# An attention and feed-forward kernel on one core: transposes moved next to scores, sums of two head pairs issued together

## What is computed

```
x = x + attn_a(layernorm(x))     # sigmoid projections Q, K, V; weights A from the means of Q and K; A @ V @ Wo + bo
x = x + ffn(layernorm(x))        # (silu(x Wg^T) * (x Wu^T)) Wd^T, hidden 384, weights are int32 times 1/127
x = x + attn_b(layernorm(x))     # 16 heads of 64, below
x = x + ffn(layernorm(x))        # the same weights again

# attn_b, per batch and head
q, k, v = x Wq + bq, x Wk + bk, x Wv + bv          # [256, 64] each
pattern = softmax(causal(q k^T / 8))               # [256, 256], upper triangle masked
out    += (pattern v) Wo                           # plus bo once
```

## Time and profile before

| what | value |
|---|---|
| runs of before | 382.17, 383.46, 384.61 us; median 383.46 us |
| the profiled execution | 382.15 us, of which 380.3 us is the span from first to last instruction |
| PE busy | 344.0 us, 90% of the span, 3208 matmuls |
| weight loads (PEld) | 277.0 us, 73% |
| DVE, ACT, POOL busy | 273.7 us (72%), 231.4 us (61%), 204.6 us (54%) |
| chain that ended last | PE 80%, DVE 6%, POOL 5%, issue 4%, ACT 2%, DMA 2% |
| mean granted TensorE clock | 0.971 of full speed |

### The profile page before, as it was taken

How to read it: one execution, slowest core, us unless ns; L and a number is a source line. 1 busy time by engine, 2 the same in 40 slices (tenths; PEclk the granted TensorE clock), 3 DMA queues, 4 the chain that set the end, 5 groups by cost and what they waited for, 6 DMA issues and landing times.

```text
span 380.3 us, 9882 instructions
## 1 busy us (share of the span) xinstructions
PE 344.0 (90%) x3208; PEld 277.0 (73%) x3208; DVE 273.7 (72%) x1084; ACT 231.4 (61%) x784; POOL 204.6 (54%) x273
## 2 busy tenths in 40 slices
PE   0366699999999999999999999999999999999865
PEld 0265578777877788778878788778887867787654
DVE  1344588897688877886888688887778697767533
ACT  2233357877486758765867658574866476658601
POOL 1616685575468635772578247753574275517420
PEclk9978899999999999999999999999999999999985
DMA  7500000000000000000000000000000000000000
GB/s 275 162 0 0 3 1 3 1 2 3 3 2 0 3 2 2 16 1 2 3 16 2 3 2 3 16 0 2 3 14 4 0 3 16 1 2 3 16 15 14
DMA packets 6418, 5.82 MB, mean 15 GB/s; under 512 B 864, under 2 KB 5856, under 8 KB 6368
## 3 DMA queue, kind: packets, MB, share of 16 engines
q1 hardware_dynamic: 5936, 3.62, 3.3%
q10 hardware_dynamic: 432, 1.57, 1.1%
HBM read 4.15 MB, written 1.05 MB: 14 GB/s over the span
## 4 chain that ended last, share of the span: by engine, by line
PE 80%; DVE 6%; POOL 5%; issue 4%; ACT 2%; DMA 2%; ACTq 0%; POOLq 0%; DVEq 0%
PE bank L380 11%; PE bank L224 10%; PE bank L359 8%; PE bank L294 7%; PE bank L346 7%; PE bank L308 7%; PE bank L344 6%; PE bank L225 6%; PE bank L226 6%; PE bank L284 4%; PE bank L285 3%; PE bank L242 2%; PE bank L273 2%; DMA wqkv<-wqkv_in 2%; POOL wqkv_lo L697 1%
## 5 line engine op out<-in xcount | busy, mean ns | idle before, releaser
L710 POOL TENSOR_TENSOR prob<-prob,row_inv 128x256 f32<-128x256 f32 (+1 forms) x128 | 103.1, 827 | 103.1 <-DVE row_inv L627 103.1
L471 ACT ACTIVATE prob<-neg_s,neg_max 128x256 f32<-128x256 f32 x128 | 63.9, 499 | 0.0
L478 ACT ACTIVATE prob_t<-bank 128x384 f32<-128x384 f32 x64 | 31.5, 492 | 39.5 <-PE bank L359 38.9
L613 DVE CUSTOM_DVE_ANT_0 neg_s<-bank,mask 128x256 f32<-128x256 f32 x128 | 53.4, 417 | 0.0
L637 DVE TENSOR_TENSOR qk<-bank,bqk 128x512 f32<-128x512 f32 x64 | 43.9, 686 | 10.2 <-PE bank L226 10.0
L469 ACT ACTIVATE prob<-neg_s,neg_max 128x128 f32<-128x128 f32 x128 | 50.6, 395 | 0.0
L620 DVE COPY prob_t<-bank 128x384 f32<-128x384 f32 x64 | 35.5, 554 | 18.9 <-PE bank L359 18.5
L380 PE MATMUL bank<-prob_t,v 128*64 128x256 f32 (+1 forms) x512 | 48.9, 332 | 0.0
L380 PEld LDWEIGHTS bank<-prob_t,v 128*64 128x64 f32 x512 | 31.8, 136 | 19.5 <-issue 10.0
L224 PE MATMUL bank<-rt_hi,wqkv_hi 128*128 128x256 f32 x128 | 42.5, 332 | 1.0 <-DVE rt_lo L586 0.9
L359 PEld LDWEIGHTS bank<-ident,prob 64*128 64x128 f32 x768 | 28.9, 138 | 14.9 <-issue 10.3
(11 more groups left out here) (135 smaller groups left out, 781.9 us busy)
## 6 DMA issues: line engine op xcount, KB each, us to landing
wqkv<-wqkv_in ACTq DMA_DIRECT2D x3, 512.0 KB, 5.4
x<-x_in SPq DMA_DIRECT2D x8, 128.0 KB, 5.7
out<-x SPq DMA_DIRECT2D x8, 128.0 KB, 1.8
wo<-wo_in SPq DMA_DIRECT2D x1, 512.0 KB, 4.7
wa<-wa_in SPq DMA_DIRECT2D x1, 192.0 KB, 6.8
wg_i<-wg_in SPq DMA_DIRECT2D x1, 192.0 KB, 5.8
wu_i<-wu_in SPq DMA_DIRECT2D x1, 192.0 KB, 5.8
wd_i<-wd_in SPq DMA_DIRECT2D x1, 192.0 KB, 5.9
```

The lines of the kernel that those rows point to most:

```text
L471: nc.scalar.activation(prob[:, r, e, P:SC], neg_s[:, m % 2, e, P:SC], ACT.Exp, bias=neg_max[:, q, 2 * e + 1:2 * e + 2], scale=-1.0, accum_ ...
L613: nc.vector.tensor_tensor_reduce(out=neg_s[:, m % 2, e, P:SC], in0=S[:, P:SC], in1=mask[:], scale=-SCORE_SCALE, scalar=3e38, op0=ALU.add, ...
L710: nc.gpsimd.tensor_tensor(pr, pr, inv, ALU.mult).then_inc(p_norm, 1)
```

## The change

The transposes of m move on PE to the scores of m+2 (2.045 instead of 2.693 in the table): for an odd m they follow these scores directly, for an even m one `sum` stands between. Scores get two PSUM banks of their own and transposes two; the ring and the waits that it needed are gone. The sum of an odd step m does the matmuls of m-1 and m together, and the result takes a turn in bank 1 of G (`take("sum", m)`) where it had z_ps to itself; `pv_done` and `z_sb` become that bank's full and free counts. All times in the tables are drawn anew, so side jobs move by some places, and so does which bank of G a job uses. For steps 24 to 26 the order on PE becomes

The number of matmuls, their shapes, and the work of the other engines are unchanged. The diff (left out are most rows of JOBS):

```
--- before.py
+++ after.py
@@ -33,7 +33,6 @@
 FC = F // P
 U = H // 2
 LAST = B * U
-LAG = 2
 SC = N + P
 HALF = 512
 HALVES = (slice(0, A), slice(A, P))
@@ -46,44 +45,44 @@
 
 
 HEADS = {
-    "PE": {"qk": -1.278, "scores": 0.0, "transposes": 2.693, "sum": 3.069},
-    "ACT": {"exp1": 0.39, "exp0": 0.465, "pt0": 2.199, "z": 2.767},
-    "DVE": {"qk": -1.106, "mask": 0.271, "inverse": 1.471, "pt1": 2.768},
-    "POOL": {"norm": 3.377},
+    "PE": {"qk": -1.313, "scores": 0.0, "transposes": 2.045, "sum": 3.01},
+    "ACT": {"exp1": 0.471, "exp0": 0.639, "pt0": 1.988, "sum": 2.727},
+    "DVE": {"qk": -0.869, "mask": 0.53, "inverse": 1.577, "pt1": 2.671},
+    "POOL": {"norm": 4.775},
 }
 JOBS = {
...
-    "POOL": {"lnsA": -13.523, "sv": -10.311, "stdp": -8.267, "lnsF": -6.527, "lnsB": -2.301, "bo": 8.947, "lnsP": 16.052},
...
+    "POOL": {"lnsA": -12.191, "sv": -7.951, "stdp": -6.381, "lnsF": -4.946, "lnsB": -1.068, "bo": 9.541, "lnsP": 16.209},
 }
 ONCE = {
-    "PE": {"bo": -7.196},
-    "ACT": {"w0": -19.802, "w1": -17.798, "w3": -14.741, "w5": -10.773, "w2": -5.195, "w4": -4.286},
-    "DVE": {"bv": -12.471, "bo": -6.68},
-    "POOL": {"w0": -22.399, "w1": -12.777, "w2": -2.943, "w3": -1.872, "w4": 0.687, "w5": 2.435},
+    "PE": {"bo": -8.324},
+    "ACT": {"w0": -18.328, "w1": -15.329, "w3": -13.411, "w4": -11.381, "w5": -9.462, "w2": -8.193},
+    "DVE": {"bv": -8.887, "bo": -3.165},
+    "POOL": {"w0": -22.179, "w1": -12.109, "w5": -4.077, "w2": -1.805, "w3": -0.176, "w4": 2.76},
 }
-BANK = {"qk": 0, "lntA": 3, "qkv0": 0, "qkv1": 1, "qkv2": 3, "mean": 2, "vwo": 1, "aout": 2, "lntF": 2, "gF0": 2, "gF1": 3, "gF2": 1,
-        "dnF": 2, "lntB": 2, "v0": 0, "v1": 1, "v2": 1, "v3": 3, "bo": 3, "out0": 1, "out1": 3, "lntP": 3, "gP0": 2, "gP1": 3, "gP2": 0,
-        "dnP": 3}
+BANK = {"qk": 0, "sum": 1, "lntA": 1, "qkv0": 3, "qkv1": 1, "qkv2": 2, "mean": 3, "vwo": 3, "aout": 2, "lntF": 3, "gF0": 2, "gF1": 3,
+        "gF2": 1, "dnF": 2, "lntB": 2, "v0": 2, "v1": 1, "v2": 1, "v3": 3, "bo": 0, "out0": 3, "out1": 2, "lntP": 3, "gP0": 1, "gP1": 3,
+        "gP2": 2, "dnP": 2}
 
 
 EARLY = ("lnsA", "lntA", "qkv0", "qkv1", "qkv2", "sv", "mean", "dist", "sign", "stdp", "vwo", "aout", "lnsF", "lntF", "gF0", "gF1", "gF2", "dnF")
-START = [0, 7.97, 16.07, 24.07, 32.01, 40.05, 48.03, 56.07]
+START = [0, 8.1, 16.07, 24.08, 32.07, 40.04, 48.03, 56.06]
 
 
 def order(engine):
 
     steps = []
     for name, at in HEADS[engine].items():
-        steps += [((m | 1 if name == "sum" else m) + at, name, m) for m in range(LAST)]
+        steps += [(m + at, name, m) for m in range(LAST) if name != "sum" or m % 2]
     for name, at in JOBS[engine].items():
         steps += [((START[b] if name in EARLY else U * b) + at, name, b) for b in range(B)]
     for name, at in ONCE[engine].items():
@@ -152,7 +151,7 @@
         zt = sb("zt", [P, 2, U, N])
 
         bank = [ctx.enter_context(nc.psum_tensor(f"bank{i}", [P, 512], F32)) for i in range(8)]
-        ring, z_ps, G = bank[0:3], bank[3], bank[4:8]
+        s_banks, t_banks, G = bank[0:2], bank[2:4], bank[4:8]
 
 
         ld_x = [sem(f"ld_x{b}") for b in range(B)]
@@ -172,7 +171,7 @@
 
         s_full, s_masked, p_inv, p_norm = sem("s_full"), sem("s_masked"), sem("p_inv"), sem("p_norm")
         p_exp = [sem("p_exp0"), sem("p_exp1")]
-        pt_full, pt_sb_a, pt_sb_b, pv_done, z_sb = (sem(n) for n in ("pt_full", "pt_sb_a", "pt_sb_b", "pv_done", "z_sb"))
+        pt_full, pt_sb_a, pt_sb_b = (sem(n) for n in ("pt_full", "pt_sb_a", "pt_sb_b"))
         stored = sem("stored")
 
         def full(eng, job, n):
@@ -185,12 +184,6 @@
 
         def home(job):
             return G[BANK[job]], g_full[BANK[job]], g_free[BANK[job]]
-
-        def s_bank(m, e):
-            return ring[(4 * m + e) % 3]
-
-        def t_bank(m, e):
-            return ring[(4 * (m + LAG) + 2 + e) % 3]
 
         def queries(m, h):
 
@@ -302,7 +295,7 @@
                     last.then_inc(done, 1)
                 elif job in ("out0", "out1"):
                     j = int(job[3])
-                    pe.wait_ge(z_sb, U // 2 * (b + 1))
+                    freed(pe, "sum", U * (b + 1) - 1)
                     take(job, b)
                     for u in range(U):
                         last = nc.tensor.matmul(out[:, 0:D], zt[:, b % 2, u, j * P:(j + 1) * P], wo[:, u, :], start=(u == 0), stop=(u == U - 1))
@@ -337,51 +330,49 @@
                 freed(pe, "qk", m)
                 if m:
                     pe.wait_ge(s_masked, 2 * m)
-                if m > LAG:
-                    pe.wait_ge(pt_sb_a, m - LAG)
                 r = m % 3
                 for e, half in enumerate(HALVES):
-                    nc.tensor.matmul(s_bank(m, e)[:, 0:P], qk[half, r, 0, 0:P], qk[half, r, 1, 0:P], start=True, stop=True)
+                    nc.tensor.matmul(s_banks[e][:, 0:P], qk[half, r, 0, 0:P], qk[half, r, 1, 0:P], start=True, stop=True)
                 for e, half in enumerate(HALVES):
-                    nc.tensor.matmul(s_bank(m, e)[:, P:SC], qk[half, r, 0, P:N], qk[half, r, 1, :], start=True, stop=True).then_inc(s_full, 1)
+                    nc.tensor.matmul(s_banks[e][:, P:SC], qk[half, r, 0, P:N], qk[half, r, 1, :], start=True, stop=True).then_inc(s_full, 1)
 
             def transposes(m):
 
                 pe.wait_ge(p_norm, 2 * m + 2)
                 if m:
+                    pe.wait_ge(pt_sb_a, m)
                     pe.wait_ge(pt_sb_b, m)
-                if m + LAG < LAST:
-                    pe.wait_ge(s_masked, 2 * (m + LAG) + 1)
                 for e in range(2):
                     for j in range(3):
                         for h, half in enumerate(HALVES):
                             at = (3 * e + j) * A
-                            last = nc.tensor.transpose(t_bank(m, h)[:, at:at + A], prob[half, m % 3, e, j * P:(j + 1) * P], ident[half, half])
+                            last = nc.tensor.transpose(t_banks[h][:, at:at + A], prob[half, m % 3, e, j * P:(j + 1) * P], ident[half, half])
                             if e == 1 and j == 2:
                                 last.then_inc(pt_full, 1)
 
-            def weighted_sum(m):
+            def weighted_sums(m):
 
                 b, u = divmod(m, U)
+                out, done, _ = home("sum")
                 pe.wait_ge(pt_sb_a, m + 1)
                 pe.wait_ge(pt_sb_b, m + 1)
-                if u == 0:
+                if u == 1:
                     freed(pe, "v0", b)
                     freed(pe, "v1", b)
-                if u == U // 2:
+                if u == U // 2 + 1:
                     freed(pe, "v2", b)
                     freed(pe, "v3", b)
-                if m % 2 == 0 and m:
-                    pe.wait_ge(z_sb, m // 2)
-                t = m % 2 * N
-                for k, cols in ((0, slice(0, N)), (1, slice(N, SC))):
-                    for e, half in enumerate(HALVES):
-                        h = 2 * u + e
-                        last = nc.tensor.matmul(z_ps[half, t + k * P:t + N], v[:, b % 2, k, h * A:(h + 1) * A], prob_t[:, m % 4, e, cols],
-                                                start=(k == 0), stop=(k == 1), skip_group_check=True)
-                last.then_inc(pv_done, 1)
-
-            steps = {"scores": scores, "transposes": transposes, "qk": projections, "sum": weighted_sum}
+                take("sum", m)
+                for i in (m - 1, m):
+                    t = i % 2 * N
+                    for k, cols in ((0, slice(0, N)), (1, slice(N, SC))):
+                        for e, half in enumerate(HALVES):
+                            h = 2 * (i % U) + e
+                            last = nc.tensor.matmul(out[half, t + k * P:t + N], v[:, b % 2, k, h * A:(h + 1) * A], prob_t[:, i % 4, e, cols],
+                                                    start=(k == 0), stop=(k == 1), skip_group_check=True)
+                last.then_inc(done, 1)
+
+            steps = {"scores": scores, "transposes": transposes, "qk": projections, "sum": weighted_sums}
             for name, n in order("PE"):
                 if name in steps:
                     steps[name](n)
@@ -441,7 +432,7 @@
                     src, _, free = home(job)
                     full(act, job, b)
                     if b >= 2:
-                        act.wait_ge(pv_done, U * (b - 1))
+                        full(act, "sum", U * (b - 1) - 1)
                     nc.scalar.activation(v[:, b % 2, j, g * HALF:(g + 1) * HALF], src[:], ACT.Copy).then_inc(free, 1)
                 elif job[0] == "w" and job != "vwo":
                     i = int(job[1])
@@ -474,25 +465,25 @@
             def pt_evac(m):
                 act.wait_ge(pt_full, 2 * m + 1)
                 if m >= 4:
-                    act.wait_ge(pv_done, m - 3)
-                nc.scalar.activation(queries(m, 0), t_bank(m, 0)[:, 0:SC].rearrange("p (k s) -> p k s", s=A), ACT.Copy).then_inc(pt_sb_a, 1)
+                    full(act, "sum", m - 4 | 1)
```

(38 more changed lines are left out.)

63 lines of the change are left out of this document (28 added, 35 removed), and 6 rows, old and new, of the table JOBS.

## The result

The changed kernel takes 368.8 us (368.5 to 371.21, 4 runs), before 384.03 us in the same comparison: a ratio of 0.962 (95% interval 0.956 to 0.968). In a second comparison it took 371.22 us beside 383.22, a ratio of 0.967 (0.963 to 0.972). The forecast was 371 us, with a range of 368.5 to 378. The profiled execution took 371.21 us, the slowest of its four, with a span of 369.4.

What follows compares the result with a forecast made beforehand. PE was taken as busy throughout, bound by what it issues, including 0.15 to 0.19 us per change of form. Savings of 13.2 us less 0.5 and 0.3 gave 12.4, so 383.46 became 371 us; range 368.5 to 378.

Steps and rivals of the forecast that it cites:

- The tolls: On PE, 44 fewer entries into whole-array form save 8.4 us and 32 fewer into transposes 4.8, together 13.2 us.
- step 0 and misfits: Costs set against the saving: 0.5 us for transposes0 waiting for norm0, 0.3 us for small misfits in 60 steps.
- the masks: PE's waits for masks between first and last scores: 0.6 us at most would go, taken as 0.
- The seam: Passage on PE from scores directly to transposes: 0.06 us at the lower end, 0.21 at the upper; the lower was taken.
- The rival with the bare weight loads: Transposes' weight loads, 0.139 us each, lie bare after scores, so 4.8 us stay: 375.9 us; chance 0.09.
- transposes25: Tightest place for PE behind norm in a period: margin 1.3 us, or 0.7 if a gate job delays DVE; cost 0.
- transposes28: Among steps 27 to 31 of a period, said to leave 1.1 us or more behind norm; cost 0.
- the walk: The new order laid against durations for one period, to find margins of transposes behind norm; cost 0.
- Both rivals with late norms: Transposes wait for POOL every period: one norm late, 383.5 us, chance 0.07; two late, 396 us, chance 0.05.
- the one with bank 1: DVE at gF2 and ACT at copies 0.7 us later, PE stalls, 6 us lost: 377 us; chance 0.10.
- From scores63 on: The kernel's end, bound by latency: sum62 waits for a copy, other jobs offset it; net 0, between -0.5 and +1.
- The start: Up to scores0: sv.1 goes behind lnsB.0 and a weight split on POOL; scores0 stay at 48.7 us, within 0.5.

## Why the prediction was right

**The tolls.** The mechanism was right: 8.4 + 4.8 us were forecast for 44 and 32 changes of form fewer, and the job put between shows what they cost. From the first to the last scores before took 302.72 us and after 290.36: 12.4 us less, to the tenth what was forecast. That precision is luck, since two terms were off by as much in opposite directions. PE's busy time fell by 11.7 us (301.47 to 289.76) and not by 13.2. Its idle time fell by 0.65 us (1.25 to 0.60), where 0.8 more had been put down for step 0 and misfits and nothing for waits that go. One of those waits the prediction didn't count at all; it gave the masks as the only one in these 303 us, but before had a second:

```profile
PE bank L242 <- POOL xn_F L672: 0.4, 1, 0.4
```

In a period the tolls gave 1.61 us and not 1.74. Of that 0.13 us the new order costs 0.11 in every period at one place: `qk` now stands right behind `mean`, whose last matmuls (L250) have one column, and its first matmul costs 0.23 us for 0.12. Before, scores stood there and cost their usual 0.42.

```profile
183.61 0.34 PE bank L250 x4
183.95 0.23 PE bank L217
```

The seam was taken at its lower end, 0.06, and the chain shows 0.37 for twelve transposes. The rival with the bare weight loads (375.9 us) is refuted by that piece.

**Waits.** (The times of this paragraph are differences of starts and ends in the trace of the kernel after.) Transposes behind norm cost 0.5 us at step 0 and nothing after, as forecast. At transposes25, told as the tightest place, norm ended 1.0 us ahead (forecast 0.7 to 1.3). In truth transposes28 are tighter, 0.65 us where I had told 1.1 or more: still enough, but the walk was off by half a microsecond there, and it is this step and those like it where putting all sums last ran dry. Both rivals with late norms, and the one with bank 1, are out by PE's single line of waits. The runs show that they weren't idle fears: with half of the transposes 1.45 us earlier, waits for norm (7.9 us) and for the later copies (4.4 us) take back what was gained there, and a poorly chosen bank costs 17.8 us of waiting.

**Small items.** From scores52 to scores63: 46.55 us before, 44.41 after, 2.1 less. Six entries into the whole array and five into transposes fewer make 1.9; PE's busy time fell by 1.6 and 0.6 of idle time went. From scores63 on: 28.86 before, 27.68 after in the profile, 29.0 in the second profile of the same kernel, so the 0 that was forecast holds within what executions of one kernel differ by. The start was told as 48.7 give or take 0.5, and it came at 51.36 and 50.68 us. That step was too narrow: I saw sv.1 behind the weight split and took it as offset, but left out that what part of this stretch runs at the lower clock (0.78 to 0.83 granted) differs between executions. For the same reason the two profiled executions are only 10.9 us apart: 12.4 less in the middle and 1.2 less at the end, but 2.6 more at the start. By medians the gain was 15.2 us in the first comparison, of four runs each, and 12.0 in the second; the forecast lies 2.2 us above the one time and 0.2 below the other. Of this scatter the prediction knew nothing, so that it met the second to 0.2 us is luck too.

**What stays open.** How much of the start after the change is order and how much clock. One execution of the five with this start came at 48.88 us, like before's 48.72, so the order doesn't force it later. But the other four came at 50.47 or later, while with the old order both profiles (before, and the one with its order and the new banks) have 48.72. The old PSUM layout with the new tables came at 48.44. Whether the new order makes the start later on average isn't settled by these. In the kernel with all sums behind transposes, some 3.5 us of the end are unexplained.

## What to carry to other kernels

When PE is busy without a gap, read the chain of waits rather than the durations: the first matmul behind a change between whole-array form, row tiles (here 64 rows) and column tiles (64 columns) shows its toll there (here 0.15 to 0.19 us), and counting such changes in the old and the new program order gave the gain in PE's time to within 1.5 of 13.2 us. To place two parts of the same form side by side, they need PSUM banks that don't wait for each other's readers, and enough distance from whoever feeds them: measure that margin step by step, and exchange only where it is larger than what the exchange takes.

## What had not been expected of the hardware

Twelve row-tiled transposes directly behind row-tiled scores add no more than in the middle of a stretch (0.37 us, six pairs at 0.062), although each of their weight loads lasts 0.139 us. The same transposes behind a wait of a microsecond add 0.59 us: here a start behind a wait cost more than a change of form (0.52). And in the same form, the first matmul of 256 columns behind `mean`'s matmuls of one column cost 0.23 us for 0.12, while behind fp32 matmuls of 128 columns it cost 0.12.
